# Attention in a seven-stage kernel: weighted sums in two halves, maxima turned on VectorE, sums inverted on GpSimd, output by feature, loads in portions

## What is computed

```python
scores = jnp.einsum('bqhd,bkhd->bhqk', Q, K) / np.sqrt(HEAD_DIM).astype(np.float32)
slopes = 0.5 ** jnp.arange(NUM_HEADS, dtype=jnp.float32)
scores = scores + slopes[None, :, None, None] * rel[None, None, :, :]
attn = jax.nn.softmax(scores, axis=-1)
out = jnp.einsum('bhqk,bkhd->bqhd', attn, V).reshape(bsz, seq_len, EMBED_DIM)
out = lora_linear(out, Wo, bo, Ao, Bo)
```

## Time and profile before

| | |
|---|---|
| median of 3 runs | 5588.35 us (5585.58 to 5592.8) |
| the profiled execution: time, span | 5591.86 us, 5590.3 us |
| TensorE, VectorE busy over the span | 91%, 77% |
| ScalarE, GpSimd busy over the span | 56%, 22% |
| setup and project | 0 to 297 us |
| attend | 297 to 3184 us |
| mix | 3184 to 3891 us |
| scan, route, expert | 3891 to 5590 us |

### The profile page before, as it was taken

One profiled execution on the slowest core, in us unless ns is written; L12 is line 12 of the kernel. 1 busy time (PEld: TensorE's weight loads), 2 busy tenths in 40 slices (PEclk: granted clock), 3 DMA queues, 4 the chain that ended last, 5 costly groups with the idle time before them and its releaser, 6 DMA issues. The chain is left out here.

```text
span 5590.3 us, 90374 instructions
## 1 busy us (share of the span) xinstructions
PE 5076.6 (91%) x27025; PEld 2738.6 (49%) x27025; DVE 4284.0 (77%) x6749; ACT 3128.3 (56%) x5877; POOL 1234.8 (22%) x959
## 2 busy tenths in 40 slices
PE   5849999999999999999999889987899999956998
PEld 3723333333333333333333367775565565645666
DVE  4758888888888888888888777887898888973000
ACT  1317778777777778777877622332454454432111
POOL 1310000000000000000000033333566656643222
PEclk8959999999999999999999889998889989956999
DMA  4850222112222022220222111112000000044443
GB/s 142 289 115 11 35 57 34 38 24 35 57 35 45 17 35 57 35 52 10 35 58 35 56 31 45 34 44 67 14 19 22 21 19 22 21 138 141 149 148 102
DMA packets 226889, 327.80 MB, mean 59 GB/s; under 512 B 58515, under 2 KB 176526, under 8 KB 216696
## 3 DMA queue, kind: packets, MB, share of 16 engines
q1 hardware_dynamic: 214300, 264.56, 19.9%
q0 software_dynamic: 12224, 58.43, 2.8%
HBM read 195.90 MB, written 134.59 MB: 59 GB/s over the span
## 5 line engine op out<-in xcount | busy, mean ns | idle before, releaser
L672 DVE TENSOR_REDUCE at_mxp<-at_ps_m 128x2 f32<-128x1024 f32 x2098 | 2463.5, 1220 | 343.0 <-PE at_ps_m L731 337.4
L622 ACT ACTIVATE at_prob<-at_ps_s 128x512 f32<-128x512 f32 x4100 | 2115.2, 602 | 479.5 <-PE at_ps_s L721 477.5
L721 PE MATMUL at_ps_s<-at_qs,at_ks 51*128 51x512 f32 x4100 | 1434.2, 474 | 13.0 <-ACT at_prob L622 2.0
L721 PEld LDWEIGHTS at_ps_s<-at_qs,at_ks 51*128 51x128 f32 x4100 | 571.3, 184 | 1258.1 <-ACT at_prob L622 1127.4
L739 PE MATMUL at_ps_o<-at_prob,at_vs 128*32 128x512 f32 x8192 | 1094.2, 606 | 0.0
L731 PE MATMUL at_ps_m<-at_ks,at_qs 49*128 49x512 f32 x4196 | 953.0, 427 | 82.1 <-DMA at_vs<-t_v 52.4
L556 POOL TENSOR_TENSOR at_onorm<-at_otok,at_rec 128x256 f32<-128x256 f32 x65 | 40.3, 620 | 2242.4 <-DVE at_rec L687 2242.4
L731 PEld LDWEIGHTS at_ps_m<-at_ks,at_qs 49*128 49x128 f32 x4196 | 423.7, 188 | 170.7 <-DVE at_mxp L672 82.5
L1205 PE MATMUL mi_ps_f<-mi_w,mi_act 128*128 128x256 f32 x1024 | 261.9, 401 | 58.9 <-DVE mi_acc L1038 58.9
L2319 ACT ACTIVATE ex_hid<-ex_ps_h,ex_b 128x512 f32<-128x512 f32 x128 | 88.0, 687 | 389.0 <-PE ex_ps_h L2335 380.7
L739 PEld LDWEIGHTS at_ps_o<-at_prob,at_vs 128*32 128x32 f32 x8192 | 161.3, 108 | 256.0 <-ACT at_prob L622 189.9
(11 more groups left out here) (310 smaller groups left out, 6299.0 us busy)
## 6 DMA issues: line engine op xcount, KB each, us to landing
t_parts<-pr_parts SPq DMA_DIRECT2D x64, 512.0 KB
ex_w<-in_fw SPq DMA_DIRECT2D x32, 1024.0 KB
at_qs<-t_parts SPq DMA_DIRECT2D x102, 256.0 KB
at_ks<-t_parts SPq DMA_DIRECT2D x102, 256.0 KB
t_buf<-at_blank POOLq DMA_DIRECT2D x8, 3076.0 KB, 9.2
at_vs<-t_v SPq DMA_DIRECT2D x17, 1024.0 KB
ex_rest<-t_buf SPq DMA_DIRECT2D x16, 1026.0 KB
t_v<-pr_vaug SPq DMA_DIRECT2D x64, 256.0 KB, 4.9
```

Source lines behind the costliest of these rows:

```text
L622: nc.scalar.activation(prob[0 if n is None else (t + 1) % 2][:, j, :], bank[:, :], ACT.Exp).then_inc(s_read, 1)
L672: nc.vector.tensor_reduce(out[:, s4, k + i, 2 * pair:2 * pair + 2], ps_m[i][:, :, :], AX.X, ALU.max).then_inc(mx_read, 1)
L721: nc.tensor.matmul(bank[:, :], ks[s][a:a + QROWS, j // 2, t1 * P:(t1 + 1) * P], qs[s][a:a + QROWS, j // 2, c * T:(c + 1) * T], start=True, ...
```

## The change

- **Weighted sums in two halves.** `weighted` is called twice a turn, for 256 queries each, once after the first two scores and the first pair for the maxima, and once at the end of the turn. The second pair for the maxima no longer has its order turned.
- **Maxima turned on VectorE.** VectorE transposes the 128x32 table of cut maxima in blocks of 32x32 at turn 8 (`turn`). The table goes to DRAM (`largest`) with one DMA and comes back as rows with four. The transposes on TensorE and the copy on ScalarE go.
- **Sums inverted on GpSimd.** `ps_o` is copied out as before. Four DMAs spread the four rows of sums over 128 partitions x 16 (`shift_sums`), GpSimd raises them to the power -1, one DMA writes them to DRAM (`inverse`), and four DMAs bring each head's row back to 16 partitions (`spread_weights`). GpSimd multiplies 128x512, and four DMAs store the result by feature (`store_rows`). The transposes to tokens, the copy and the reciprocal go.
- **Output by feature.** Mix loads the output already transposed. `attention_rows` goes on TensorE and ScalarE. bv is added in project instead, where VectorE adds it with four instructions of 128x256 a chunk in place of two copies.
- **Loads in portions.** A unit's operands come one band (four DMAs of 256 KB) in each of the first three chunks, and the values in the fourth. The values have a semaphore of their own. The buffer is cleared with one DMA of 393 KB a chunk.
- The loop bodies span four units, and the ring of `ps_s` holds scores alone.

```diff
-                    nc.vector.tensor_copy(vaug[h][:, 2 * half:2 * half + 2, :, 0:HD],
-                                          ps_v[half][:, :, :].rearrange("p s (h e) -> p s h e", e=HD)).then_inc(v_out, 1)
+                    for s in range(2):
+                        last = nc.vector.tensor_tensor(vaug[h][:, 2 * half + s, :, 0:HD], ps_v[half][:, s, :].rearrange("p (h e) -> p h e", e=HD),
+                                                       bv[:, :].rearrange("p (h e) -> p h e", e=HD), ALU.add)
+                    last.then_inc(v_out, 1)
...
+                    pool.wait_ge(sums_in, 16 * HPG * (n + 1))
+                    nc.gpsimd.tensor_tensor(total[:, :], total[:, :], minus[:, :], ALU.pow).then_inc(inverted, 1)
+                    pool.wait_ge(weight_in, 16 * HPG * (n + 1))
+
+                    pool.wait_ge(o_stored[r], 16 * HPG * m)
+                    nc.gpsimd.tensor_tensor(onorm[r][:, :], osum[:, :], weight[:, :], ALU.mult).then_inc(norm_done, 1)
+
...
+                        nc.gpsimd.dma_start(d["buf"][ds(n * P, P), :], blank[:, :]).then_inc(cleared, 16)
...
+                def load_band(u, s, r):
                     b, g = u // G, u % G
-                    for r, (qp, kp) in enumerate(CUTS):
-                        for dst, part, row in ((qs, qp, 0), (ks, kp, HPG * HD)):
-                            src = d["parts"][ds(g, 1), part, row:row + HPG * HD, ds(b * S, S)].rearrange("g (i a e) t -> a e (g i) t", a=2, e=HD)
-                            for a in range(2):
-                                sp.dma_start(dst[s][a * 64 + r * HD:a * 64 + (r + 1) * HD, :, :].bitcast(F32), src[a]).then_inc(kq_in[s], 16)
+                    for dst, part, row in ((qs, CUTS[r][0], 0), (ks, CUTS[r][1], HPG * HD)):
+                        src = d["parts"][ds(g, 1), part, row:row + HPG * HD, ds(b * S, S)].rearrange("g (i a e) t -> a e (g i) t", a=2, e=HD)
+                        for a in range(2):
+                            sp.dma_start(dst[s][a * 64 + r * HD:a * 64 + (r + 1) * HD, :, :].bitcast(F32), src[a]).then_inc(kq_in[s], 16)
+                    if r == 0:
+                        for j in range(HPG):
+                            sp.dma_start(ks[s][j % 2 * 64 + ALI:j % 2 * 64 + ALI + 1, j // 2, :].bitcast(F32), d["alibi"][ds(g * HPG + j, 1), :]).then_inc(kq_in[s], 16)
+
+                def load_values(u, s):
+                    sp.dma_start(vs[s][:, :, :], d["v"][ds(u, 1), :, :, :].rearrange("u p k c -> p (u k) c")).then_inc(v_in[s], 16)
+
+                def shift_sums(n):
+                    wait_alone(sp, o_out, n + 1, always)
...
+                        sp.dma_start(total[32 * j:32 * j + 32, :], osum[32 * j + HD:32 * j + HD + 1, :].rearrange("p (k x) -> p k x", x=HD)).then_inc(sums_in, 16)
+
+                def spread_weights(n, r):
+                    wait_alone(sp, inverted, n + 1, always)
+                    sp.dma_start(d["inverse"][r].rearrange("j (k x) -> (j k) x", x=HD), total[:, :]).then_inc(inverse_out, 16)
+                    wait_alone(sp, inverse_out, 16 * (n + 1), always)
                     for j in range(HPG):
-                        sp.dma_start(qs[s][j % 2 * 64 + MXR:j % 2 * 64 + MXR + 2, j // 2, c * T:(c + 1) * T].bitcast(F32), nrows[2 * j:2 * j + 2, :].bitcast(F32)).then_inc(max_in, 16)
+                        sp.dma_start(weight[32 * j:32 * j + HD, :], d["inverse"][r, j, :].partition_broadcast(HD)).then_inc(weight_in, 16)
+
+                def store_rows(n, r):
+                    wait_alone(sp, norm_done, n + 1, always)
+                    for j in range(HPG):
+                        sp.dma_start(d["o"][ds(n, 1), j * HD:(j + 1) * HD, :].rearrange("n p q -> (n p) q"), onorm[r][32 * j:32 * j + HD, :]).then_inc(o_stored[r], 16)
...
+                def store_max(n, r, s, c):
+
+                    wait_alone(sp, turned, n + 1, always)
+                    sp.dma_start(d["largest"][r].rearrange("k (w x) -> w k x", w=4), nturned[:, :]).then_inc(turned_out, 16)
+                    wait_alone(sp, turned_out, 16 * (n + 1), always)
+                    for j in range(HPG):
+                        row = j % 2 * 64 + MXR
+                        sp.dma_start(qs[s][row:row + 2, j // 2, c * T:(c + 1) * T].bitcast(F32),
+                                     d["largest"][r][j * 2 * SUB:(j + 1) * 2 * SUB, :].rearrange("(e s) q -> e (s q)", e=2)).then_inc(max_in, 16)
...
+                            shift_sums(n)
+                            spread_weights(n, c % 2)
+                            if c < len(CUTS):
+
+                                load_band((u + 1) % UNITS, 1 - s, c)
+                            else:
+                                load_values((u + 1) % UNITS, 1 - s)
+                            store_rows(n, c % 2)
+                            store_max(n + 1, (c + 1) % 2, s if c < QC - 1 else 1 - s, (c + 1) % QC)
...
                 def take_sums(n):
 
+                    act.wait_ge(norm_done, n)
                     act.wait_ge(o_done, n)
                     nc.scalar.copy(osum[:, :], ps_o[:, :]).then_inc(o_out, 1)
...
+                def turn(n):
+
+                    dve.wait_ge(turned_out, 16 * n)
+                    dve.wait_ge(neg_cut, n + 1)
+                    nc.vector.transpose(nturned[:, :], nparts[:, :, :, :].rearrange("p j e s -> p (j e s)").bitcast(F32)).then_inc(turned, 1)
...
-                def max_scores(n, s, c, t, i, order=(0, 1)):
+                def max_scores(n, s, c, t, i):
 
                     s4, pair, k = tile(t)
                     if not (isinstance(n, int) and n * MXN + 2 * t + i < 2):
                         pe.wait_ge(mx_read, n * MXN + 2 * t + i - 1)
                     q0 = c * T + s4 * P
-                    for a in order:
+                    for a in range(2):
                         last = nc.tensor.matmul(ps_m[i][:, a, :], qs[s][a * 64:a * 64 + MXR, pair, q0:q0 + P],
                                                 ks[s][a * 64:a * 64 + MXR, pair, (k + i) * T:(k + i + 1) * T], start=True, stop=True)
...
+                def weighted(up, r, s, t, half):
+
+                    q0, q1 = half * T // 2, (half + 1) * T // 2
+                    if half == 0:
+                        pe.wait_ge(s_read, HPG + up * LOOP + (r * KT + t) * HPG)
                     for j in range(HPG):
-                        last = nc.tensor.matmul(ps_o[32 * j:32 * j + 32, :], vs[s][:, t, 32 * j:32 * j + 32], prob[t % 2][:, j, :],
-                                                start=(t == 0), stop=(t == KT - 1), tile_position=(0, 32 * j), skip_group_check=True)
-                    if t + 1 == KT:
+                        last = nc.tensor.matmul(ps_o[32 * j:32 * j + 32, q0:q1], vs[s][:, t, 32 * j:32 * j + 32], prob[t % 2][:, j, q0:q1],
+                                                start=(t == 0 and half == 0), stop=(t == KT - 1), tile_position=(0, 32 * j), skip_group_check=True)
+                    if half and t + 1 == KT:
                         last.then_inc(o_done, 1)
...
+                            if (mc, t) == (QC, NEXT):
+
+                                pe.wait_ge(kq_in[1 - s], 16 * NLD * (up * (LU // 2) + (uu + 1) // 2 + 1))
+                            if t + 1 == KT:
+
+                                pe.wait_ge(max_in, 16 * HPG * (n + 2))
+                            scores(up, r, t, 0, *nxt)
+                            scores(up, r, t, 1, *nxt)
+                            max_scores(*best, 0)
+                            if t == 0:
+
+                                pe.wait_ge(o_out, n + 1)
+                                if c == 0:
+                                    pe.wait_ge(v_in[s], 16 * (up * (LU // 2) + uu // 2 + 1))
+                            weighted(up, r, s, t, 0)
+                            scores(up, r, t, 2, *nxt)
+                            scores(up, r, t, 3, *nxt)
+                            max_scores(*best, 1)
+                            weighted(up, r, s, t, 1)
...
+                        p = g % 2 * HPG * HD
+                        sp.dma_start(oT[h][p:p + HPG * HD, g // 2, :], d["o"][ds((b * G + g) * CPB + c + 1, 1), :, :].rearrange("n p q -> (n p) q")).then_inc(o_in[h], 16)
...
-                def attention_rows(n):
-                    act.wait_ge(tro_done, n + 1)
-                    for k in range(KD):
-                        last = nc.scalar.activation(oT[:, k, :], ps_t[k][:, :], ACT.Identity, bias=keep["bvT"][:, k:k + 1])
-                    last.then_inc(oT_done, 1)
...
+        "o": ([UNITS * (S // T) + 1, HPG * HD, T], F32),
+        "inverse": ([2, HPG, T], F32),
+        "largest": ([2, HPG * 2 * SUB, P], F32),
```

More of the change, by code:

```diff
@@ L508, in attend_phase @@
         kq_in = [sem(f"kq_in{s}") for s in range(2)]
+        v_in = [sem(f"v_in{s}") for s in range(2)]
         ones_set = [sem(f"ones_set{s}") for s in range(2)]
@@ L593, in _ @@
                 sp.wait_ge(ones_set[0], 1)
-                load(0, 0)
+                for r in range(len(CUTS)):
```

(20 more changed lines are left out.)

257 lines of the change are left out of this document (91 added, 166 removed).

## The result

The changed kernel takes 5644.08 us (median of 4 runs, 5631.18 to 5654.26) against 5589.26 us (4 runs). The ratio is 1.0098, with a 95% interval of 1.0077 to 1.0119: 1% slower, where 5442 us and 2.6% faster was forecast. The profiled execution has a span of 5651.9 us against 5590.3, and a mean granted clock of 0.892 against 0.931.

What follows compares the result with a forecast made beforehand. A loop of TensorE and ScalarE through the ring of three banks was taken to bound attend's turn. Terms -252 + 98 - 8 + 13 + 5 - 2 = -146 us gave a median of 5442 us, range 5330 to 5630.

Steps and rivals of the forecast that it cites:

- The forecast case: Whole kernel: attend's turn falls to 2.43 us, TensorE stalls in every unit, total 5442 us; chance 0.5.
- the switch costs its full price: Rival in attend: entering `weighted` costs 0.43 us, turn 2.65, chunk 42.7, total 5638 us; chance 0.2.
- The turn: Attend: two half-turns of 1.22 us make 2.43 instead of 2.61; chunk 39.2 us, -252 us over 63 chunks.
- the wait for ScalarE: Attend, old order: the fourth score waits for head 0's exponential, costing 0.50 us a turn, which the split removes.
- The stall's length: Attend, turn 7 of each unit's third chunk: TensorE waits 4.1 us for the third band, landing at 21.4 us.
- The clock behind the stall: Attend: half-clock stretches after each stall cost 2 us more a unit; with the stall +98 us over 16 units.
- Start and end: Attend's start, with fewer loads to await, gains 8 us; its end, with SyncE's chain now serial, loses 13.
- Project: Project: four evacuations take 1.66 us where two copies took 1.27, on TensorE's path; +5 us.
- Mix: Mix: removing eight transposes, all but about 0.1 us hidden beside a ScalarE copy, gains 2 us.
- Clearing in portions: Buffer cleared in 64 portions: same bytes on another queue, nothing waits; 0 us.
- SyncE late: Rival in attend: SyncE's chain overruns by more than 9 us, delaying maxima or weights; about 5760 us, chance 0.1.
- no stall: Rival in attend: the third band lands by 17.3 us, so TensorE never waits; 5344 us, chance 0.2.

Runs made afterwards that it cites:

- the version with both repairs: Changed kernel with bands 2 and 3 loaded in a unit's second chunk and eight idle transposes in mix: 5423.63 us, ratio 0.9703 to the kernel before.

## Why the prediction was wrong

The forecast case was the right one of the four: a shorter turn and a stall at turn 7 of each third chunk. Its sum was -146 us and came out at +61.6 in the profiled execution. The measured 5644 us lies close to the 5638 of the rival in which the switch costs its full price, but that is chance: its turn of 2.65 did not come. By its own steps:

- **The turn.** Forecast 2.43, measured 2.48; the wait for ScalarE is gone, as said. The cost of going to and from `weighted` was sized right (0.33 for 0.32, 0.57 for 0.56), and the 0.02 of each half-turn add up. Chunk 40.0 for 39.2, so -202 us over 63 chunks for -252: 50 us of the miss. One sign did not come: VectorE shows no 0.1 us of idle time before each reduction (three of them take 3.71 us, 1.24 each, and not 1.134), yet the run with shorter reductions shows that it does not bound the turn. The Trainium skill's 60 cycles for each matmul (TensorEngine Tiling (Array Packing), Instruction Overhead), from which the prediction estimated a turn of 2.63, charged the eight extra matmuls too much here; the trace shows 2.48.
- **The stall's length.** Forecast 4.1 us a unit, measured 5.0 (79.8 us in all): +14. The band was issued at 12.0 us for 11.9 and landed 1.5 us later than my 21.4, in the unit shown. Right in kind and nearly in size. (The fast end of 19.5 does not follow from the steps named for it; they give about 20, which changes nothing.)
- **The clock behind the stall: the step that failed.** I wrote "one to two such stretches cost 1.4 to 2.8 us. I take 2". It was 7.5. I took the length of the low stretch from one row in mix and carried it into attend. Attend before had one such gap of its own, in its first chunk, and I left it out:

```profile
423.40 0.80 PE L731 MATMUL at_ps_m<-at_ks,at_qs 49*128 49x512 f32 x2 [8.75 <-DVE at_mxp L672]
```

The granted clock was 0.50 for 7.7 us behind it, which would have priced the clock at about 3 us a unit. Even that is short: behind the band's gaps the lower level lasts 8.7 to 28 us. Why it lasts so much longer there than in mix, and why it varies, no run shows. Filling the gap with work took the 7.5 us away and left the 5. This is 16 x 5.5 = 88 us of the miss, and with the turn it eats the whole gain of attend. The upper end (9 us a unit, +144) was below the measured +200 too.
- **Start and end.** Forecast -8 and +13, measured -10 (start -0.6, first chunk -9.0) and +14. Over the versions with the split the first chunk took 47.3 to 59.9 us, mostly with the same code in its path, so the -8 was met in part by luck. **Project** with setup: +5, measured +5.7, of which 1.3 lie in setup. In the other versions, with the same code there, it is +2 to +5.5, so this agreement too is partly luck.
- **Mix: the second step that failed.** I wrote "eight transposes in 1.27 us, beside a ScalarE copy that TensorE must wait for anyway" and took -2. The copy did hide them, so removing them gained nothing. But they kept TensorE busy just behind a low stretch. Without them the stage takes 755.2 us, 48.7 more than before; with idle ones in their place it takes 704.3. I had costed the edit in busy time, not in what it does to the clock: 51 us of the miss.
- **Clearing in portions**: "nothing waits: 0". Route lost 10.3 us, 8 of them by this; what the other 2 come from is open.
- **SyncE late, full switch, no stall**: none happened. Rows of maxima were never waited for, and no wait for them shows at turn 15.

Together: 50 + 14 + 88 + 51 + 10, less the 4.7 of scan, is 208, the distance from -146 to +62. Most of it, 139 us, is one error twice: TensorE's standing still was priced with little or nothing for the low clock behind it.

## What to carry to other kernels

Where TensorE bounds a stage, price each new gap on it by the low clock behind it as well as by its length, and take the stretch from 3 us up to 30, as here, since it can be far longer than the gap and differs from one gap to the next. Before removing work from TensorE, look whether it stands between two waits: work that is hidden behind a copy may still hold the clock, and some idle transposes in a gap of a few us can gain more than they cost. In a queue that runs in order, put the transfer that has a due time ahead of the round trips that have none.

## What was unexpected of the hardware

- After a gap of 4 to 6 us in attend, TensorE stayed at 1.2 GHz for 8.7 to 28 us more, in one unit recorded busy without a break (24.00 of 24 us at a granted 0.51). In mix a gap of 3.36 us was followed by 3.4 us at that level with work between the waits, and by up to 13.7 us without.
- Gaps of 1.4 to 3.1 us brought the lower level in 11 of 14 cases: in all eight of 1.83 us and more, and in three of six below. In one run 1.52 us brought 17 us of it, 1.70 and 1.76 us nothing; in the version with both repairs a gap of 1.89 us brought nothing either.
- 64 DMAs of 0.4 MB from GpSimd instead of 8 of 3 MB raised the idle time before the indirect stores of a stage some 1700 us later from 39.9 to 68.1 us.
